# Routed experts: eleven batches routed early instead of twelve, list ends on the sync queue, late scatters three to a unit, and the 176 inner columns in two halves of 88

## The chip, the cores and the metric

The kernel runs on one core of one Trainium2 chip. The metric is the device time of one execution in microseconds, the median of several runs. The program is written as one instruction stream per engine (TensorE, VectorE, ScalarE, GpSimd and SyncE), which wait for each other by semaphores.

## The reference, cut to what matters

The reference is a decoder of two layers on 16 batches of 128 tokens of width 256. Layer 0 has attention, cross attention and a feed-forward; layer 1 has windowed attention, cross attention and routed experts. The change touches the last part and, through its first steps, the two attentions ahead of it.

```python
shared_out = silu_and_mul(xf @ shared_w1.T) @ shared_w2.T        # inner width 352
probs = softmax(xf @ gate_w.T)                                   # 16 experts
routing_weights, selected = top_k(probs, 6)
gate_up = einsum('th,eoh->teo', xf, w1)                          # inner width I = 176 for each expert
act = silu(gate) * up
moe_out = einsum('te,tei,ehi->th', combine, act, w2)
x = layernorm(x + moe_out + shared_out)
```

There are 2048 tokens, each goes to 6 of the 16 experts.

## The kernel before, in words

All values are float32. The routed part is not computed densely. Every expert has a list of token rows in memory (`spread`); a token's row (its 256 values, its number and its 16 weights, 273 values) is written to six lists by indirect transfers, six scatters for a batch of 128 tokens. Then 111 tiles of 128 rows are read back from the lists, each tile belongs to one expert, and its result is added into memory by an indirect transfer that accumulates.

There are three stages at the end of the program.

1. *The two small attentions* (`small_attentions`, function `overlapped`). The orders of the pieces on each engine are written out by hand in `SELF_ORDERS` and `CROSS_ORDERS` (lines 1675 to 1701), as names with a lag in batches. `EarlyRouting` puts the router of batches 0 to 11 there, in three groups of four: logits, six best, positions in the lists (class `Router`), and the scatters (`scatter0` to `scatter5`, line 2497) on GpSimd. At the stage's end SyncE waits for all scatters, and all engines meet at a barrier (line 109).
2. *The shared stage* (first part of `routed_feed_forward`). Four groups of four batches pass the shared expert in three units each (128, 128 and 96 of 352 columns), twelve units `q`. TensorE makes gate and up (line 3162), ScalarE the silu (3266), VectorE the product (3351), TensorE projects (3173) two units later. Between groups TensorE turns the next tokens (3143) and ScalarE copies them out (3253). The router of the last four batches runs beside it (lines 2281 to 2360); GpSimd then issues 24 scatters (3115) and 16 list ends (3119), indirect transfers that fill the 128 slots behind each list with empty rows. `tables` and `tables_back` (3319 to 3343) work out which expert and which rows each tile has.
3. *The tile loop*, 111 tiles. SyncE reads the rows (3095). TensorE works in rounds: turn the rows of tile i (3203), gate and up of tile i-1 (3217), turn the product of tile i-2 (3225, 3226), result of tile i-3 (3232, 3233). The inner width of 176 stands across partitions as 128 + 48: two transposes, two copies out (3402, 3403), and two matmuls that accumulate:

```python
pe.matmul(p_y[i % 2][:, 0:H], actT[i % 2][:, :], weights.w2[:, bass.ds(e * H, H)], start=True, stop=False)
pe.matmul(p_y[i % 2][:, 0:H], actT_low[i % 2][:, :], weights.w2_low[:, bass.ds(e * H, H)],
          start=False, stop=True).then_inc(y_made, 1)
```

GpSimd adds the result into one of two buffers in memory in turn (3127) and waits before each for the one two tiles earlier to have landed (`done_of(i - 2)`). A float32 matmul is two passes, so the trace has two instructions for one `matmul` call.

Of the kernel before, what the change touches and what calls it, by code (L numbers as in the profile page):

```python
# [1273 lines left out]
def x0_attend(core, kT, svu, rsv, vraw, ahead):  # L1274
# [10 lines left out]
    with ExitStack() as ctx:  # L1285
# [323 lines left out]
        def _(dve):  # L1609
# [620 lines left out]
EI, SI = 176, 352  # L2230
GROUP = 4
# [7 lines left out]
EARLY = 3  # L2239


class Router:

    SIZES = (("logit", GROUP * EXPERTS), ("prob", GROUP * (EXPERTS + 2)), ("repl", GROUP * (EXPERTS + 2)),
             ("chosen", GROUP * EXPERTS), ("order", GROUP * EXPERTS), ("count0", GROUP * (PAD + EXPERTS)),
             ("count1", GROUP * (PAD + EXPERTS)), ("slotf", GROUP * EXPERTS), ("pick", CHOICES * GROUP * EXPERTS),
             ("slot", CHOICES * GROUP), ("info", GROUP * (1 + EXPERTS)), ("rstat", 3 * GROUP), ("best", GROUP * 8))
    ROOM = sum(n for _, n in SIZES)  # L2250
    STEPS = 1 + 4 + 1 + GROUP + 1 + 1 + 1

    def __init__(self, core, weights, sem, room, first, groups):
        self.core, self.weights, self.first, self.groups = core, weights, first, groups
        at = {}
        for name, n in self.SIZES:
            lo = sum(m for _, m in self.SIZES[:len(at)])
            at[name] = room[:, lo:lo + n]

        def by_group(name):  # L2260
            return at[name].rearrange("p (g e) -> p g e", g=GROUP)
# [5 lines left out]
        self.pick = at["pick"].rearrange("p (k g e) -> p k g e", k=CHOICES, g=GROUP)  # L2267
        self.slot_all, self.slot = at["slot"], at["slot"].rearrange("p (k g) -> p k g", k=CHOICES)
# [4 lines left out]
            "c_steps", "info_up", "slots_up"))  # L2273

# [5 lines left out]
    def shifted(self, dve, n, logits):  # L2280
        dve.tensor_reduce(self.rstat[:, 0, :], logits, AX.X, ALU.max).then_inc(self.r_max, 1)
        dve.wait_ge(self.r_max, n + 1)
        dve.tensor_tensor(self.logit, logits, bcast(self.rstat[:, 0, :], [P, GROUP, EXPERTS]), ALU.subtract).then_inc(self.r_in, 1)

    def exponentials(self, act, n):
        act.wait_ge(self.r_in, n + 1)
        act.wait_ge(self.ready, 3)
        after(act, self.info_up, n)
        act.activation(self.prob[:, :, 0:EXPERTS], self.logit, ACT.Exp).then_inc(self.r_exp, 1)

    def choose(self, dve, n):
        rstat, prob, repl, best = self.rstat, self.prob, self.repl, self.best
        pr = prob[:, :, 0:EXPERTS]
        dve.wait_ge(self.ready, 3)
        dve.wait_ge(self.r_exp, n + 1)
        dve.tensor_reduce(rstat[:, 1, :], pr, AX.X, ALU.add).then_inc(self.r_steps, 1)
        dve.wait_ge(self.r_steps, 3 * n + 1)
        dve.reciprocal(rstat[:, 2, :], rstat[:, 1, :]).then_inc(self.r_steps, 1)
        dve.wait_ge(self.r_steps, 3 * n + 2)
        dve.tensor_tensor(pr, pr, bcast(rstat[:, 2, :], [P, GROUP, EXPERTS]), ALU.mult).then_inc(self.r_steps, 1)  # L2300
# [3 lines left out]
        for j in range(GROUP):  # L2304
            dve.wait_ge(self.r_best, GROUP * n + j + 1)
            dve.match_replace(repl[:, j, :], best[:, j, :], prob[:, j, :], CHOSEN).then_inc(self.r_repl, 1)
        dve.wait_ge(self.r_repl, GROUP * (n + 1))
        dve.tensor_scalar(self.chosen, repl[:, :, 0:EXPERTS], CHOSEN, None, ALU.is_ge).then_inc(self.chosen_up, 1)

    def describe(self, dve, n):  # L2310

        lo = (self.first + n) * GROUP
        dve.tensor_copy(self.info[:, :, 0], self.weights.token[:, lo:lo + GROUP])
        dve.scalar_tensor_tensor(out=self.info[:, :, 1:], in0=self.repl[:, :, 0:EXPERTS], scalar=CHOSEN, in1=self.prob[:, :, 0:EXPERTS],
                                 op0=ALU.is_ge, op1=ALU.mult).then_inc(self.info_up, 1)

    def rank(self, pe, n, bank):
        pe.wait_ge(self.chosen_up, n + 1)
        m = GROUP * EXPERTS
        pe.matmul(bank[:, 0:m], self.weights.earlier[:, :], self.picked, start=True, stop=True)  # L2320
        pe.matmul(bank[:, m:2 * m], self.weights.every[:, :], self.picked, start=True, stop=True).then_inc(self.ranked, 1)

    def positions(self, dve, n):

        at = self.STEPS * n
        dve.wait_ge(self.chosen_up, n + 1)
        dve.tensor_copy(self.count[0][:, :, PAD:], self.chosen).then_inc(self.c_steps, 1)
        for i, s in enumerate((1, 2, 4, 8)):
            dve.wait_ge(self.c_steps, at + 1 + i)
            dve.tensor_tensor(self.count[(i + 1) % 2][:, :, PAD:], self.count[i % 2][:, :, PAD:],  # L2330
                              self.count[i % 2][:, :, PAD - s:PAD + EXPERTS - s], ALU.add).then_inc(self.c_steps, 1)
        dve.wait_ge(self.c_steps, at + 5)
        dve.tensor_tensor(self.order, self.count[0][:, :, PAD:], self.chosen, ALU.mult).then_inc(self.c_steps, 1)

    def take(self, dve, n, bank):

        base, at, w, lo = self.weights.base, self.STEPS * n + 6, GROUP * EXPERTS, (self.first + n) * GROUP
        dve.wait_ge(self.weights.ones_up, 2)
        dve.wait_ge(self.ranked, n + 1)
        for j in range(GROUP):  # L2340
# [3 lines left out]
        dve.tensor_tensor(self.slotf, base[:, lo:lo + GROUP, :], bank[:, 0:w].rearrange("p (g e) -> p g e", e=EXPERTS),  # L2344
# [1170 lines left out]
```

## Time and profile before

| | us |
|---|---|
| runs, median of 3 | 2864.49 (2857.27 to 2869.05) |
| the profiled execution | 2860.28 |
| its span | 2858.4 |
| mean granted clock of TensorE | 0.933 |
| TensorE busy | 2400.8 (84%) |
| VectorE busy | 1886.4 (66%) |
| ScalarE busy | 1596.1 (56%) |
| GpSimd busy | 733.2 (26%) |

Times in the profile are microseconds from the span's start. PE is TensorE's matmuls, PEld its weight loads, DVE VectorE, ACT ScalarE, POOL GpSimd, SPq SyncE's queue. "<-" behind an instruction's idle time names what ended it; "issue" is time in which nothing that is recorded held it, "remote" a release that no recorded instruction explains. The small attentions end at 2382.6, the shared stage runs from there to 2503, the tile loop to about 2823, and the last sums and norms to the end. The share of busy time over the whole span tells little here, since each stage is limited by something else; the stretches and chains below are to be read stage by stage.

### The profile page before, as it was taken

The page shows a single profiled execution, that of the slowest core. Times are in us where ns is not written, and L with a number is a line of the kernel's source. Part 1 is how long each engine was busy: PE and PEld are TensorE (multiplying, and loading weights), DVE is VectorE, ACT ScalarE, POOL GpSimd, SP SyncE. Part 2 cuts the span into 40 slices and gives each one's busy share as a digit, 9 for nine tenths or more (in the row PEclk, how much of TensorE's full clock was granted, in tenths as well). Part 3 has the DMA queues.
Part 4 walks back from the last instruction along what each step waited for, and adds up shares of the span by engine and source line. Part 5 has one row for each costly group of instructions (what it writes and reads, how often), then busy time and mean ns, then how long its engine had stood idle before and what let it go on. Part 6 is the DMA issues. An engine that isn't in the chain of part 4 may idle for free. (4 is left out here: it accounts for less than half of the span.)

```text
span 2858.4 us, 50647 instructions
## 1 busy us (share of the span) xinstructions
PE 2400.8 (84%) x16545; PEld 1519.7 (53%) x16545; DVE 1886.4 (66%) x4500; ACT 1596.1 (56%) x3092; POOL 733.2 (26%) x913
## 2 busy tenths in 40 slices
PE   6999999999976577777777799799979765599995
PEld 3766667676753344444444455455556543355552
DVE  5778787777747899999999322466657652134443
ACT  3666665656643799989999311466646541033332
POOL 1121212121201222222222000111112664245554
PEclk9999999999997899989999899999999987799997
DMA  5000000000000899999999500400000113156665
GB/s 191 1 1 0 0 0 0 0 0 0 0 23 23 173 186 184 181 173 188 178 179 184 115 1 0 142 1 1 1 7 12 65 64 106 54 96 97 98 97 135
DMA packets 537921, 211.18 MB, mean 74 GB/s; under 512 B 475012, under 2 KB 531840, under 8 KB 536704
## 3 DMA queue, kind: packets, MB, share of 16 engines
q1 hardware_dynamic: 515952, 178.30, 31.0%
q0 software_dynamic: 21360, 30.22, 6.0%
q8 instruction: 113, 1.85, 0.3%
q14 instruction: 80, 0.66, 0.1%
q10 hardware_dynamic: 416, 0.16, 0.0%
HBM read 54.27 MB, written 36.90 MB: 32 GB/s over the span
## 5 line engine op out<-in xcount | busy, mean ns | idle before, releaser
L1651 DVE TENSOR_SCALAR_CACHE_REDUCE x_row<-x_p_s,x_nsq 128x1024 f32<-128x1024 f32 x512 | 621.7, 1274 | 28.7 <-PE x_p_s L1427 28.7
L1520 ACT ACTIVATE x_ints<-x_row,x_nb 128x2048 uint16<-128x2048 f32 x256 | 511.7, 2000 | 41.9 <-DMA x_turned<-x_ints 20.7
L1427 PE MATMUL x_p_s<-x_kT,x_qz 128*128 128x512 bf16 x1024 | 321.0, 409 | 131.5 <-DVE x_row L1651 126.9
L363 POOL TENSOR_TENSOR a_rstd<-a_ssq,neghalf 128x16 f32<-128x16 f32 x32 | 126.0, 3936 | 522.0 <-DVE a_ssq L874 522.0
L3127 POOL DMA_INDIRECT f_acc<-f_yt,f_ids x111 | 171.9, 1548 | 201.9 <-ACT f_yt L3290 200.6
L1427 PEld LDWEIGHTS x_p_s<-x_kT,x_qz 128*128 128x128 bf16 x1024 | 72.3, 101 | 268.0 <-DVE x_row L1651 242.1
L1554 POOL TENSOR_SCALAR x_nb<-x_low,x_hmin 128x1 f32<-128x1 f32 x256 | 75.0, 293 | 498.4 <-DVE x_row L1651 497.1
L1461 PEld LDWEIGHTS x_p_o<-x_vi,x_turned 128*128 128x128 f16 x4096 | 144.0, 98 | 87.2 <-DMA x_turned<-x_ints 18.3
L2095 ACT COPY s_eT<-sc_p_e 128x512 f32<-128x512 f32 x192 | 112.3, 585 | 132.4 <-PE sc_p_e L1985 131.5
L1461 PE MATMUL x_p_o<-x_vi,x_turned 128*128 128x16 bf16 x4096 | 143.0, 170 | 17.1 <-DMA x_turned<-x_ints 17.0
L3217 PE MATMUL f_p_g<-f_w,f_rowsT 128*128 x444 | 151.0, 463 | 0.0
L1985 PE MATMUL sc_p_e<-ident,s_e 128*128 128x128 f32 x768 | 124.4, 286 | 30.6 <-ACT s_eT L2095 17.6
L3402 DVE COPY f_actT<-f_p_u 128x128 f32<-128x128 f32 x111 | 32.4, 291 | 170.2 <-issue 149.9
L704 ACT ACTIVATE a_prob<-a_p_work,a_nbias,a_rqs 128x128 f32<-128x128 f32 x256 | 114.3, 463 | 36.7 <-DVE a_nbias L983 36.7
L1985 PEld LDWEIGHTS sc_p_e<-ident,s_e 128*128 128x128 f32 x768 | 86.1, 144 | 75.6 <-issue 58.4
L450 PE MATMUL a_p_proj<-a_wq,a_xT 128*128 128x512 f32 x256 | 123.7, 608 | 2.7 <-DMA a_wq<-in_L_attn_Wq_dram 2.7
L570 PE MATMUL a_p_o<-a_wo,a_cT 128*128 128x256 f32 x512 | 120.9, 379 | 0.0
L450 PE MATMUL a_p_proj<-a_wk,a_xT 128*128 128x512 f32 x256 | 117.6, 593 | 0.0
L2889 DVE TENSOR_TENSOR f_h<-f_act_g,f_p_u 128x512 f32<-128x512 f32 x32 | 22.0, 688 | 138.1 <-PE f_p_y L2791 123.3
L450 PE MATMUL a_p_proj<-a_wv,a_xT 128*128 128x512 f32 x256 | 112.7, 592 | 0.3 <-ACT a_cv L663 0.3
L2083 ACT ACTIVATE s_e<-s_e 128x1024 f32<-128x1024 f32 x96 | 100.1, 1059 | 13.5 <-DVE s_e L2181 10.8
L2172 DVE TENSOR_REDUCE s_rmax<-sc_p_s 128x8 f32<-128x1024 f32 x64 | 76.6, 1217 | 45.3 <-PE sc_p_s L1968 45.3
(462 smaller groups left out, 5484.7 us busy)
## 6 DMA issues: line engine op xcount, KB each, us to landing
f_rows<-f_spread SPq DMA_DIRECT2D x111, 136.5 KB
f_w<-in_L_ffn_w_dram SPq DMA_DIRECT2D x2, 2816.0 KB, 13.1
x_turned<-x_ints SPq DMA_TRANSPOSE x224, 4.8
f_sum<-f_acc SPq DMA_DIRECT2D x6, 512.0 KB, 7.1
x_res<-in_x_dram SPq DMA_DIRECT2D x2, 1024.0 KB, 7.1
a_wq<-in_L_attn_Wq_dram SPq DMA_DIRECT2D x2, 1024.0 KB, 10.8
a_wk<-in_L_attn_Wlk_dram SPq DMA_DIRECT2D x1, 2048.0 KB, 18.5
a_wv<-in_L_attn_Wlv_dram SPq DMA_DIRECT2D x1, 2048.0 KB, 10.8
```

The source lines that it names most:

```text
L363: pool.tensor_tensor(rstd[:, hs], ssq[:, hs], core.neghalf[:, 0:NH], ALU.pow).then_inc(root_h.sem, 1)
L450: mm = pe.matmul(proj[n % 2][:, :], xT[:, t, :], w_qkv[i][:, t, c * BANK:(c + 1) * BANK], start=(t == 0), stop=(t == KT - 1))
L570: mm = pe.matmul(p_o[:, 0:H], cT[g % 2][:, h, :], w_o[:, g * G + h, :], start=(g == 0 and h == 0), stop=(g == NG - 1 and h == G - 1))
L704: i = act.activation(prob[g % 2][:, h, :], work[g % 2][:, h * P:(h + 1) * P], ACT.Exp, bias=nbias[:, n:n + 1], scale=rqs[:, n:n + 1], accu ...
L1427: mm = pe.matmul(p_s[n % SLOTS][:, c * BANK:(c + 1) * BANK], qz[b % 2][:, par, a, :], kT[:, a, at:at + BANK], start=True, stop=True)
L1461: mm = pe.matmul(p_o[:, h * XD:(h + 1) * XD], turned[k][:, c, :].bitcast(F16), vi[:, c, h * XD:(h + 1) * XD], start=(c == 0), stop=(c == B ...
L1520: act.activation(ints[k][:, :], rows[k][:, :, :].rearrange("p s n -> p (s n)"), ACT.Exp, bias=nb[:, k:k + 1], scale=-1.0, accum_out=esum[: ...
L1651: dve.tensor_scalar(rows[k][:, half, :], p_s[n % SLOTS][:, :], nsq[:, b % 2, h:h + 1], HIGHEST, ALU.mult, ALU.min, accum_out=(low if half ...
L1985: mm = pe.transpose(s.p_e[:, j * P:(j + 1) * P], s.e[(b * s.PAIRS + g // 2) % 4][:, g % 2 * G + j, :], core.ident[:, :])
L2095: act.copy(s.eT[g % 4][:, :, :].rearrange("p g k -> p (g k)"), s.p_e[:, :]).then_inc(s.eT_up.sem, 1)
L3127: pool.indirect_dma_start(acc[i % 2], bass.IndirectOffsetOnAxis(ap=ids[i % YR][:, :], axis=0), yt[i % YR][:, :], None, compute_op=ALU.add) ...
L3217: mm = pe.matmul(p_g[i % 2][:, 0:2 * EI], rowsT[i % 2][:, t * P:(t + 1) * P], weights.w1[:, t, bass.ds(e * (2 * EI), 2 * EI)], start=(t == ...
```

## The change

Four things are changed together.

- `SPANS` replaces groups of equal size: groups of 4, 4 and 3 batches are routed in the small attentions, the last five batches in the shared stage. The logits of batch 11 are still made early and kept in `left`. In GpSimd's order the six scatters of a batch stand two, two and two instead of three, one, one and one. Six scatters fewer are issued early, six more late.
- The 16 list ends move from GpSimd's indirect transfers to SyncE: plain transfers whose address is read from a register.
- The 30 late scatters wait for the gates of the units, three for each (`paced`). The ranking matmuls move from behind unit 1 to behind unit 0, and numbering stands ahead of the first product; the tables are read back at unit 9 instead of 11.
- The 176 inner columns are held as two halves of 88: weights, transposes and matmuls have 88 partitions each, and one copy of 88x256 replaces two.

```diff
+HALF = EI // 2
-EARLY = 3
+SPANS, REST = ((0, 4), (4, 4), (8, 3)), (11, 5)
...
-    "pool": [("spread1", 1), ("scatter3", 9), ("residual", 0), ("root_qk", 0), ("scatter4", 9), ("spread0", 0), ("scatter5", 9),
-            ("norm_root", 3), ("scatter0", 8), ("scatter1", 8), ("scatter2", 8)],
+    "pool": [("spread1", 1), ("scatter2", 9), ("scatter3", 9), ("residual", 0), ("root_qk", 0), ("scatter4", 9), ("scatter5", 9),
+            ("spread0", 0), ("norm_root", 3), ("scatter0", 8), ("scatter1", 8)],
...
-        self.w2, self.w2_low = sb("w2", [P, EXPERTS * H]), sb("w2_low", [low, EXPERTS * H])
+        self.w2 = [sb(f"w2{j}", [HALF, EXPERTS * H]) for j in range(2)]
...
+        def paced(m):
+            return 1 + m // 3
...
             sp.dma_start(spread[EXPERTS * CAP:, :], empty[:, :]).then_inc(dump_in, 16)
+            sp.wait_ge(empty_up, 2)
+            for e in range(EXPERTS):
+                at = sp.value_load(empty_at[0:1, e:e + 1], min_val=0, max_val=SLOTS - P)
+                sp.dma_start(spread[bass.ds(at, P), :], empty[:, :]).then_inc(ends_in, 16)
...
-            for j in range(GROUP):
+            for j in range(LATE):
                 pool.wait_ge(staged_up, j + 1)
                 pool.wait_ge(router.slots_up, 1)
                 for k in range(CHOICES):
+                    pool.wait_ge(gate_made, paced(j * CHOICES + k))
...
-            pool.wait_ge(empty_up, 2)
-            for e in range(EXPERTS):
-                pool.indirect_dma_start(spread, bass.IndirectOffsetOnAxis(ap=empty_at[:, e:e + 1], axis=0),
-                                        empty[:, :], None).then_inc(ends_in, 16)
...
+                if not q:
+                    router.rank(pe, 0, p_x[1])
                 if q >= 2:
                     project(q - 2)
-                if q == 1:
-                    router.rank(pe, 0, p_x[1])
-                if q == total - 1:
+                if q == total - 3:
                     turn_tables()
...
-                pe.transpose(p_u[i % 2][:, 0:P], act_in[i % 2][:, 0:P], core.ident[:, :])
-                pe.transpose(p_u[i % 2][0:LOW, P:2 * P], act_in[i % 2][:, P:EI], core.ident[:, :]).then_inc(act_turned, 1)
+                for j in range(2):
+                    mm = pe.transpose(p_u[i % 2][0:HALF, j * P:(j + 1) * P], act_in[i % 2][:, j * HALF:(j + 1) * HALF], core.ident[:, :])
+                mm.then_inc(act_turned, 1)
...
-                pe.matmul(p_y[i % 2][:, 0:H], actT[i % 2][:, :], weights.w2[:, bass.ds(e * H, H)], start=True, stop=False)
-                pe.matmul(p_y[i % 2][:, 0:H], actT_low[i % 2][:, :], weights.w2_low[:, bass.ds(e * H, H)],
-                          start=False, stop=True).then_inc(y_made, 1)
+                for j in range(2):
+                    mm = pe.matmul(p_y[i % 2][:, 0:H], actT[i % 2][:, j * P:(j + 1) * P], weights.w2[j][:, bass.ds(e * H, H)],
+                                   start=(j == 0), stop=(j == 1))
+                mm.then_inc(y_made, 1)
...
-                dve.tensor_copy(actT[i % 2][:, :], p_u[i % 2][:, 0:P])
-                dve.tensor_copy(actT_low[i % 2][:, :], p_u[i % 2][0:LOW, P:2 * P]).then_inc(actT_up, 1)
+                dve.tensor_copy(actT[i % 2][:, :], p_u[i % 2][0:HALF, 0:2 * P]).then_inc(actT_up, 1)
```

The first place is one batch of the small attentions on GpSimd (c_kz at line 1866 is a "spread", x_res the residual, c_rstd and c_ln_r the two roots, the DMA rows are scatters). Before:

```order
L1852 TENSOR_TENSOR x_res<-x_res,c_bias_out 128x256
L1858 TENSOR_TENSOR c_rstd<-c_ssq,c_eps 128x2
L1860 TENSOR_TENSOR c_rstd<-c_rstd,neghalf 128x2
L2497 DMA f_spread<-s_kz,f_slots 34944x273
L1866 TENSOR_TENSOR c_kz<-c_qkT,c_owner 128x256
L2497 DMA f_spread<-s_kz,f_slots 34944x273
L1874 TENSOR_TENSOR c_ln_r<-c_mv,c_eps 128x1
L1876 TENSOR_TENSOR c_ln_r<-c_ln_r,neghalf 128x1
L2497 DMA f_spread<-s_kz,f_slots 34944x273 x3
L1866 TENSOR_TENSOR c_kz<-c_qkT,c_owner 128x256
L2497 DMA f_spread<-s_kz,f_slots 34944x273
L1852 TENSOR_TENSOR x_res<-x_res,c_bias_out 128x256
```

In the changed kernel (the lines of the scatters are 2521 there):

```order
L2521 DMA f_spread<-s_kz,f_slots 34944x273 x2
L1852 TENSOR_TENSOR x_res<-x_res,c_bias_out 128x256
L1858 TENSOR_TENSOR c_rstd<-c_ssq,c_eps 128x2
L1860 TENSOR_TENSOR c_rstd<-c_rstd,neghalf 128x2
L2521 DMA f_spread<-s_kz,f_slots 34944x273 x2
L1866 TENSOR_TENSOR c_kz<-c_qkT,c_owner 128x256
L1874 TENSOR_TENSOR c_ln_r<-c_mv,c_eps 128x1
L1876 TENSOR_TENSOR c_ln_r<-c_ln_r,neghalf 128x1
L2521 DMA f_spread<-s_kz,f_slots 34944x273 x2
L1866 TENSOR_TENSOR c_kz<-c_qkT,c_owner 128x256
```

Three scatters ahead of the second spread became two, and two stand together behind the root of q and k.

The second place is the end of the small attentions and the rest of the program on GpSimd. Before:

```order
L2497 DMA f_spread<-s_kz,f_slots 34944x273 x6
L1874 TENSOR_TENSOR c_ln_r<-c_mv,c_eps 128x1
L1876 TENSOR_TENSOR c_ln_r<-c_ln_r,neghalf 128x1
L2497 DMA f_spread<-s_kz,f_slots 34944x273 x12
L2512 UNCONDITIONAL_BRANCH
L108 ISA x3
L3108 UNCONDITIONAL_BRANCH
L3110 MEMSET f_sum 128x1024
L3115 DMA f_spread<-f_staged,f_slots 34944x273 x24
L3119 DMA f_spread<-f_empty,f_empty_at 34944x273 x16
L3127 DMA f_acc<-f_yt,f_ids 2176x256 x111
```

In the changed kernel:

```order
L2521 DMA f_spread<-s_kz,f_slots 34944x273 x6
L1874 TENSOR_TENSOR c_ln_r<-c_mv,c_eps 128x1
L1876 TENSOR_TENSOR c_ln_r<-c_ln_r,neghalf 128x1
L2521 DMA f_spread<-s_kz,f_slots 34944x273 x6
L2536 UNCONDITIONAL_BRANCH
L108 ISA x3
L3140 UNCONDITIONAL_BRANCH
L3142 MEMSET f_sum 128x1024
L3148 DMA f_spread<-f_staged,f_slots 34944x273 x30
L3156 DMA f_acc<-f_yt,f_ids 2176x256 x111
```

The last twelve early scatters became six, the 24 late ones 30, and the 16 list ends are gone from this engine.

The third place is one round of the tile loop on TensorE. Before (f_w is the wide part of the weights, f_w_low the 48 rows):

```order
L3225 MATMUL f_p_u<-ident,f_act 128x128
L3226 MATMUL f_p_u<-ident,f_act 48x128
L3232 ISA
L3232 MATMUL f_p_y<-f_w,f_actT 128x256
L3233 REGISTER_ALU
L3233 MATMUL f_p_y<-f_w_low,f_actT_low 128x256
L3203 MATMUL f_p_x<-ident,f_rows 128x128 x2
```

In the changed kernel:

```order
L3255 MATMUL f_p_u<-ident,f_act 88x128 x2
L3263 ISA
L3263 MATMUL f_p_y<-f_w,f_actT 128x256
L3263 REGISTER_ALU
L3263 MATMUL f_p_y<-f_w,f_actT 128x256
L3232 MATMUL f_p_x<-ident,f_rows 128x128 x2
```

The same number of passes stands in the same order; 128 and 48 partitions became 88 and 88.

## Rows read from the trace of the kernel before

**Rows 1.** Stretches: us, busy PE PEld DVE ACT POOL (count), clock, DMA share, GB/s.

```profile
2432.00:2453.00 21.00, 0.00 (x0) 0.00 (x0) 0.68 (x1) 0.00 (x0) 16.12 (x17) 0.50 0.30 113
2620.00:2720.00 100.00, 100.00 (x425) 59.80 (x425) 42.00 (x210) 37.29 (x106) 55.01 (x36) 1.00 0.60 97
```

**Rows 2.** Timeline of the standstill: start, us, engine, line, operation, [idle before <-releaser].

```profile
2424.75 0.59 ACT L3266 ACTIVATE f_act_g<-f_p_g 96x512 f32<-96x512 f32 x1 [10.93 <-remote]
2452.15 0.68 DVE L3351 TENSOR_TENSOR f_h<-f_act_g,f_p_u 96x512 f32<-96x512 f32 x1 [31.71 <-remote]
2459.07 1.07 ACT L3253 COPY f_xT<-f_p_x 128x512 f32<-128x512 f32 x2 [33.73 <-remote]
2460.20 3.78 PE L3162 MATMUL f_p_g<-f_xT,f_sg 128*128 128x512 f32 x4 [36.78 <-ACT f_xT L3253]
2480.45 1.98 PE L3162 MATMUL f_p_g<-f_xT,f_sg 128*128 128x512 f32 x4 [1.16 <-ACT f_xT L3253]
```

**Rows 3.** Late scatters and list ends by line: ns min/median/max, first and last start.

```profile
L3115 POOL DMA_INDIRECT f_spread<-f_staged,f_slots x24: 959/963/967, 2402.8 to 2432.0; - x24
L3119 POOL DMA_INDIRECT f_spread<-f_empty,f_empty_at x16: 959/963/964, 2433.2 to 2452.2; - x16
```

**Rows 4.** DMA queues from 2418.6 to 2424.8: packets, MB, share.

```profile
q8 instruction: 1, 0.02, 1.0%
```

**Rows 5.** Timeline of POOL and PE at the border of the two stages.

```profile
2354.51 2.07 PE L2027 MATMUL sc_p_out<-c_w_o,s_oT 128*128 128x256 f32 x4 [0.46 <-issue]
2358.84 1.17 POOL L2497 DMA_INDIRECT f_spread<-s_kz,f_slots  x1 [0.19 <-issue]
2372.99 0.96 POOL L2497 DMA_INDIRECT f_spread<-s_kz,f_slots  x1 [0.30 <-issue]
2382.58 0.95 POOL L3110 MEMSET f_sum<- 128x1024 f32 x1 [8.63 <-POOLq L109]
```

**Rows 6.** Waits from 2225 to 2340, then 2340 to 2384: us, times, longest.

```profile
PE sc_p_s L1960 <- POOL c_kz L1866: 11.3, 5, 2.6
POOL c_kz L1866 <- ACT c_qkT L2077: 13.2, 7, 3.9
ACT s_oS L2107 <- remote: 3.8, 1, 3.8
```

**Rows 7.** Timeline, start of the shared stage: the choice, and unit 1 on TensorE.

```profile
2392.00 0.20 DVE L2308 TENSOR_SCALAR f_room<-f_room 128x64 f32<-128x64 f32 x1
2394.84 1.88 PE L3162 MATMUL f_p_g<-f_xT,f_sg 128*128 128x512 f32 x4
```

**Rows 8.** Chain of waits through one round of the tile loop.

```profile
2642.07 1.19 PE f_p_g L3217 x4
2643.47 0.43 PE f_p_y L3232 x2
2643.90 0.63 PE f_p_y L3233 x2
2644.53 0.37 PE f_p_x L3203 x2
2644.90 1.19 PE f_p_g L3217 x4
```

**Rows 9.** Chain of waits in the shared stage: a projection of 96 rows.

```profile
2489.32 1.73 PE f_p_y L3173 x8
```

**Rows 10.** Timeline of the tile loop: the weight loads of 48 rows.

```profile
2621.16 0.29 PEld L3233 LDWEIGHTS f_p_y<-f_w_low,f_actT_low 48*128 48x128 f32 x2 [0.33 <-issue]
```

**Rows 11.** Chain of waits behind the loop: an accumulation into memory.

```profile
2820.71 3.99 DMA f_acc<-f_yt,f_ids
2824.76 0.69 issue
```

**Rows 12.** SyncE, row transfers at a register address: ns min/median/max.

```profile
L3094 SPq TENSOR_LOAD <-f_row_of x111: 262/268/770, 2502.0 to 2809.1; - x111
L3095 SPq DMA_DIRECT2D f_rows<-f_spread x111: 337/338/379, 2503.2 to 2809.8; - x111
```

More of the change, by code:

```diff
@@ L2273, in __init__, with earlier_ones @@
             "c_steps", "info_up", "slots_up"))
+    def earlier_ones(self, n):
+        return sum(m for _, m in self.spans[:n])
     def start(self, dve):
@@ L2382, in __init__, with span_of @@
         self.turn, self.small = other.p_out[:, H:2 * H], other.p_out[:, H:H + EXPERTS]
-        self.batches = EARLY * GROUP
+        self.batches, self.looked = REST[0], REST[0] + 1
+    def span_of(self, b):
+        return sum(b >= lo + m for lo, m in SPANS)
     def tensor(self, pe):
@@ L2398, in logits @@
         def logits(b):
-            if b < s.batches:
+            if b < s.looked:
                 if not b:
@@ L2407, in rank @@
         def rank(b):
-            if b < s.batches and b % GROUP == GROUP - 1:
+            if b in s.last:
                 pe.wait_ge(s.read, b + 1)
@@ L2411, in rank @@
                 pe.wait_ge(s.weights.ones_up, 2)
-                s.router.rank(pe, b // GROUP, s.turn)
+                s.router.rank(pe, s.last[b], s.turn)
         return {"r_turn": turn, "r_logits": logits, "r_rank": rank}
     def free(self, pe, b):
-        after(pe, self.read, min(b - 1, self.batches))
-        after(pe, self.router.taken, min((b - 6) // GROUP + 1, EARLY))
+        after(pe, self.read, min(b - 1, self.looked))
+        after(pe, self.router.taken, sum(b >= at + 3 for at in self.last))
     def scalar(self, act):
@@ L2433, in logits_up @@
         def logits_up(b):
-            if b < s.batches:
+            if b < s.looked:
                 act.wait_ge(s.made, b + 1)
-                after(act, s.router.r_in, b // GROUP)
-                act.copy(s.raw[:, b % GROUP, :], s.small).then_inc(s.read, 1)
+                n = s.span_of(b)
+                after(act, s.router.r_in, n)
+                dst = s.raw[:, b - SPANS[n][0], :] if b < s.batches else s.weights.left[:, 0, :]
+                act.copy(dst, s.small).then_inc(s.read, 1)
         def exponentials(b):
-            if b < s.batches and b % GROUP == GROUP - 1:
-                s.router.exponentials(act, b // GROUP)
+            if b in s.last:
+                s.router.exponentials(act, s.last[b])
         def stage(b):
@@ L2457, in run @@
             def run(b):
-                if b < s.batches and b % GROUP == GROUP - 1:
-                    piece(b // GROUP)
+                if b in s.last:
+                    piece(s.last[b])
             return run
@@ L3087, in _ @@
             sp.wait_ge(dump_in, 16)
-            for i in range(GROUP):
+            for i in range(LATE):
                 sp.wait_ge(spread_in[i], 16 * CHOICES)
@@ L3257, in stage @@
                 act.wait_ge(router.info_up, 1)
-                for j in range(GROUP):
-                    act.copy(staged[j][:, 0:H], core.x[:, EARLY * GROUP + j, :])
+                for j in range(LATE):
+                    act.copy(staged[j][:, 0:H], core.x[:, BEFORE + j, :])
                     act.copy(staged[j][:, H:], router.info[:, j, :]).then_inc(staged_up, 1)
@@ L3367, in _ @@
             router.positions(dve, 0)
+            router.take(dve, 0, p_x[1])
+            router.number(dve, 0)
             for q in range(total):
```

152 lines of the change are left out of this document (82 added, 70 removed).

## The prediction, made before the changed kernel ran

> **What bounds the kernel now.** I read the busy time by stretch first, then the timeline where a stretch is empty, then the chain of waits through the stage that is left. The reader is to see three different things in the last 500 us.
>
> The shared stage (all tokens through the shared expert, twelve units) has a hole. From 2432 to 2453 TensorE works 0.00 us of 21 and ScalarE not at all, while GpSimd is busy for 16 of them [rows 1]. The timeline names the instructions: ScalarE's activation of 2424.75 had waited 10.93 us, VectorE's product of 2452.15 waited 31.71, ScalarE's copy of 2459.07 waited 33.73, all "remote", which means that no recorded instruction released them; TensorE then waited 36.78 us for that copy [rows 2]. TensorE had ended its last work at 2460.20 - 36.78 = 2423.4, so the later two had their inputs 25 to 35 us before they ran. What ran meanwhile was GpSimd's row of indirect transfers: 24 scatters from 2402.8 and 16 list ends until 2452.2 [rows 3]. One fetch of instructions is recorded just before 2424.8, where ScalarE went on [rows 4]. So I take the hole as instruction pages that come late while GpSimd issues indirect transfers without a pause. That is an inference: for the two longer waits no fetch is recorded.
>
> The border before the shared stage is set by GpSimd alone. TensorE ends at 2356.58, twelve scatters start from 2358.84 to 2372.99, and the new stage starts at 2382.58 [rows 5].
>
> The tile loop is TensorE's: 100.00 us busy of 100, clock 1.00, GpSimd at 55 [rows 1]. One round is 2644.90 - 2642.07 = 2.83 us, and 111 rounds are 314 us [rows 8].
>
> **The change, part by part.** The sum is made against the profiled execution's 2860.28 us (span 2858.4), which is 4.2 us under the median of the runs, 2864.49.
>
> *Border.* Eleven batches instead of twelve are scattered early. Behind the last early root there are 6 scatters instead of 12, as the order rows show. One costs (2372.99 - 2358.84) / 11 = 1.286 us, so the border comes 6 x 1.286 = 7.7 us earlier. The last scatter then ends at about 2366.2, still behind TensorE's 2356.58, so GpSimd stays the last and the gain counts whole; the 9.6 us from the last scatter to the new stage stay. In the same place ScalarE has one "remote" wait of 3.8 us beside twelve scatters in a row [rows 6]; it may go or stay (0 to 3.8), and I take 2.
>
> *Order on GpSimd in the early part.* Three scatters before spread1 become two, and scatter 5 moves ahead of spread0. TensorE waited 11.3 us in five batches for that product of GpSimd [rows 6]; this is the most that can come back. Against it: spread0 has one more scatter ahead, 1.286 us, but GpSimd idled 13.2 / 7 = 1.9 us there waiting for ScalarE [rows 6], which covers it. Were that cover gone it would cost 11 x 1.286 = 14.1. Between -11.3 and +14.1 I take -7, near the row that shows the cover.
>
> *Shared stage.* What the hole costs: 36.78 us, less the 1.16 that every turn of a new group leaves there, and the first projection at half clock (3.78 us against 1.98) [rows 2]: 35.6 + 1.8 = 37.4 us. The clock row over the empty stretch is 0.50, so TensorE starts again at 1.2 GHz [rows 1]. The change issues the thirty late scatters three to a unit; a unit is three pieces of 1.73 us [rows 9], 5.2 us, so GpSimd issues for 3.9 us and then pauses. Six go at once at the start, since unit 1 is under way when the slots are known. The last three wait for the tenth gate of twelve, two units or 10 us before TensorE's end, against 3.99 us for an indirect transfer to land [rows 11]; nothing is late for the first tile's rows. The pacing also limits itself: a unit that stands still releases no more scatters. What stays dense is SyncE's part: sixteen list ends at 0.268 + 0.338 us or more each [rows 12], 10 to 18 us, on hardware queues and beside at most nine scatters. The bounds are 0 and -37.4; I leave 4 us of waiting and take -33.4.
>
> The rest of this stage I cost at nothing. The added waits: ranking now waits behind unit 0 for the choice, and unit 1 stands behind it on TensorE; the choice of four batches was made at 2392.2 and unit 1 started at 2394.84 [rows 7], so 2.6 us cover the fifth batch and two small copies. Behind the paced scatters GpSimd has only the accumulations, which need the first tile anyway; numbering before the first product delays that product, whose buffer TensorE wants only in unit 2; the tables and the 111 x 16 owner compare move from unit 11 to unit 9, behind nothing that TensorE waits for. If this cover were gone it would be some single microseconds. SyncE's sixteen list ends stand ahead of its stores of x, which nothing before the loop needs.
>
> *Tile loop.* In the round the two passes of 128 rows (line 3232) take 0.43 us, the two of 48 rows (line 3233) 0.63, and the two transposes behind them 0.37; the two transposes before 3232 take 2643.47 - 2643.26 = 0.21 [rows 8]. Same columns, so 0.20 and 0.16 us are extra, and they stand around the 48-row step only: its weight load starts 0.33 us after the one before ended [rows 10]. A 96-row projection in the shared stage pays nothing: eight passes in 1.73 us, 0.216 each, as fast as the 0.43 / 2 of line 3232 [rows 8, 9]. Halves of 88 rows are nearer to 96. Saved: 0.36 x 111 = 40.0 us; I take 38, because the first and last rounds are not steady. Bounds: 0, if 88 behaves as 48 (a loss is excluded, since the passes and their columns are the same), and -40.0. VectorE's one copy of 88x256 for two copies is beside the path: TensorE leaves no gap there.
>
> The page "TensorEngine Tiling (Array Packing)" of the Trainium skill (section Tiling Modes) says that a change of tiling mode drains TensorE, and lists modes of 128, 64 and 32 rows. By it 48 rows would be a 64-row mode and both 88 and 96 the full one; the rows agree as far as 48 and 96 go. No run here shows 88.
>
> Sum: 7.7 + 2 + 7 + 33.4 + 38 = 88.1; 2860.3 - 88.1 = 2772.2, and with the 4.2 to the median **2776 us**. After the loop I expect nothing to change.
>
> **Rivals.**
> A. *The hole stays, fed by SyncE.* The starving is by the amount of transfers, not by who issues them; the sixteen list ends and the first six scatters then stand closer together than before. For it: the transfers and their bytes are as many as before. Against: the DMA engines were only 0.30 busy in the hole and 0.60 in the loop, which has no such wait [rows 1]. Price: the 37.4 us stay, 2776 + 33.4 = 2809.
> Beside it, the page "DMA: Bandwidth & Descriptors" of the skill (section Issuing engines are not separate DMA queues) says that DMAs of SyncE and GpSimd end on the same 16 engines, so moving the issue saves sequencer time alone; that speaks for A. The busy share in rows 1 does not bear it out.
> B. *88 rows pay as 48 do.* The loop gives nothing: 2776 + 38 = 2814. Against it is the 96-row row.
> C. *The accumulation becomes the bound.* Each of two memory buffers takes the next tile only when its last one has landed: 3.99 + 0.69 us for two tiles [rows 11], 2.34 us per tile, against the new round of 2.47. The margin is 0.13 us. The DMA share would rise from 0.60 to 0.69; if landing grows to 4.6, the tile takes 2.65 and the loop gives 20 us: 2794.
> D. *Every burst starves the engines by itself; this is the way to a slower kernel.* ScalarE went on 6.9 us after the last list end started [rows 2, 3]. If each of ten bursts holds ScalarE and VectorE from its first scatter until then, 2 x 1.286 + 6.9 = 9.4 us, and TensorE restarts at half clock (1.8), ten bursts cost 112 us instead of 37.4. With the other terms (54.7 gained) that is 20 us slower: 2884. It decides from 9.2 us per burst. Against it: in the early part six scatters per batch, three in a row, go with no remote wait in the list of 2225 to 2340; the one of 3.8 us comes in the stretch after it [rows 6], where they stand in runs of six and twelve.
>
> **Chances.** Forecast 0.60; A 0.16; C 0.10; B 0.07; A and B together 0.04 (2847); D 0.03. The forecast's own range is 2756 (all terms at their best, 100.2 us, and the spread of the runs) to 2795. The range reaches over A and B to 2820 and leaves out the last two. A measurement of this kernel tells about 0.5% from no change, 14 us, so the limits are 2850 and 2879. Faster 0.95 (the first four and half of A with B), same 0.02, slower 0.03.
>
> **What would show it.** Border: six scatters behind the last root and the first transpose of the new stage between 2362 and 2375, near 2366. Hole: no "remote" wait above 5 us in the shared stage, and the scatters in threes. If it is still there, whether it falls beside SyncE's sixteen (A) or beside each three (D). Loop: rounds of 2.47 us in the chain, the four result passes 0.86 us together; a round of 2.83 is B, and GpSimd waiting for its own transfer is C. I am wrong in the large if the hole moves elsewhere instead of going, since that term and the loop carry 71 of the 88 us.

## The result, and the profile after

The changed kernel takes 2773.11 us (median of 4 runs, 2769.67 to 2785.46) beside 2860.88 of the kernel before: ratio 0.970, 95% interval 0.966 to 0.974. On another chip the pair was timed again: 0.969, 0.968 to 0.970. The forecast was 2776. The span of the profiled execution is 2770.3 us, so 88.1 us went, which is to the tenth the forecast's sum; the table shows that its terms missed in both directions.

| stretch | before | after | gone | forecast |
|---|---|---|---|---|
| start to the first c_rstd (L1858) of the cross attention | 2111.4 | 2114.7 | -3.3 | 0 |
| from there to the last stage's MEMSET | 271.2 | 251.9 | 19.3 | 7.7 + 2 + 7 = 16.7 |
| shared stage, to the first transposes of rows | 122.7 | 84.9 | 37.8 | 33.4 |
| tile loop, to the last ones | 309.3 | 275.8 | 33.5 | 38 |
| rest of the span | 43.8 | 43.0 | 0.8 | 0 |

The first row is no effect: the second profile of the changed kernel has 2109.2 there, that of the kernel before 2112.2.

*The border.* The timeline of the changed kernel's GpSimd answers to [rows 5]: the first and the last of the six scatters behind the last root, and the new stage at 2366.59 where it was 2382.58 (the forecast said near 2366).

```profile
2351.52 1.16 POOL L2521 DMA_INDIRECT f_spread<-s_kz,f_slots  x1 [0.19 <-issue]
2358.05 0.96 POOL L2521 DMA_INDIRECT f_spread<-s_kz,f_slots  x1 [0.30 <-issue]
2366.59 0.95 POOL L3142 MEMSET f_sum<- 128x1024 f32 x1 [7.58 <-POOLq L109]
```

*The shared stage.* The stretches of the changed kernel, with the columns of [rows 1], from the first late scatter on, and in the loop. TensorE is busy for 19 us of 21 while GpSimd issues nearly as densely as in the old hole (15 transfers and 13.89 us busy against 17 and 16.12).

```profile
2384.00:2405.00 21.00, 19.01 (x65) 11.04 (x64) 5.85 (x19) 3.45 (x6) 13.89 (x15) 1.00 0.50 172
2600.00:2700.00 100.00, 99.57 (x479) 73.21 (x478) 46.11 (x199) 38.13 (x119) 61.87 (x40) 1.00 0.65 109
```

The twelve scatters that are released at once (the slots are known only when four gates have been made) still leave a trace. In the timeline ScalarE's gate had its input from the pass of 2395.53, which ended at 2397.4. VectorE's first product had its inputs earlier still. Both engines go on together at 2400.6, 2.2 us after the twelfth issue ended. TensorE has work for that long and loses next to nothing.

```profile
2395.53 1.88 PE L3191 MATMUL f_p_g<-f_xT,f_sg 128*128 128x512 f32 x4
2400.58 0.60 ACT L3297 ACTIVATE f_act_g<-f_p_g 128x512 f32<-128x512 f32 x1 [7.70 <-DMA x_wp<-in_L_xattn_Wp_dram]
2400.62 1.33 DVE L3382 TENSOR_TENSOR f_h<-f_act_g,f_p_u 128x512 f32<-128x512 f32 x2 [12.39 <-PE f_p_u L3191]
```

The releaser "x_wp" is a load from long ago: the trace has no fitting release there either, under another name.

*The loop.* The chain of waits through one round answers to [rows 8]; the round is 2642.47 - 2639.98 = 2.49 us (forecast 2.47).

```profile
2639.98 1.19 PE f_p_g L3246 x4
2641.16 0.22 PE f_p_u L3255 x2
2641.38 0.86 PE f_p_y L3263 x4
2642.25 0.22 PE f_p_x L3232 x2
2642.47 1.19 PE f_p_g L3246 x4
```

The timeline has the weight loads of 88 rows back to back, without the idle 0.33 of [rows 10]:

```profile
2641.11 0.73 PEld L3263 LDWEIGHTS f_p_y<-f_w,f_actT 88*128 88x128 f32 x4
```

### The profile page after: what moved, and what is told of

Its sections match the earlier page's. It is cut to its first block and busy times, and to the rows that moved or that the text cites. A ratio compares the mean times of both kernels' runs of the same rounds, so it can differ in the third digit from the quotient of the medians.

```text
span 2770.3 us, 50620 instructions
## 1 busy us (share of the span) xinstructions
PE 2359.1 (85%) x16545; PEld 1537.1 (55%) x16545; DVE 1883.0 (68%) x4391; ACT 1585.0 (57%) x3092; POOL 715.0 (26%) x897
## 5 line engine op out<-in xcount | busy, mean ns | idle before, releaser
L3436 DVE COPY f_actT<-f_p_u 88x256 f32<-88x256 f32 x111 | 46.7, 421 | 130.8 <-PE f_p_u L3255 97.8
L3263 PE MATMUL f_p_y<-f_w,f_actT 88*128 x444 | 114.2, 379 | 0.0
L2083 ACT ACTIVATE s_e<-s_e 128x1024 f32<-128x1024 f32 x96 | 100.0, 1058 | 13.3 <-DVE s_e L2181 12.5
## 6 DMA issues: line engine op xcount, KB each, us to landing
a_wq<-in_L_attn_Wq_dram SPq DMA_DIRECT2D x2, 1024.0 KB, 11.3
```

What stands on the lines that cost most here:

```text
L3263: mm = pe.matmul(p_y[i % 2][:, 0:H], actT[i % 2][:, j * P:(j + 1) * P], weights.w2[j][:, bass.ds(e * H, H)], start=(j == 0), stop=(j == 1))
```

## Experiments

Times compare with the kernel before on the same chip. The chips were of two kinds, which was not expected. On at least three of them, and where the first two profiles come from, the kernel before takes 2854 to 2870 us, on two others 2814 to 2829. I call them chips of kind 1 and kind 2. Each was used in one short stretch of time only, so what differs may lie in the chip or in something else that held for that stretch.

### What makes the hole

Five kernels differ in how many indirect transfers GpSimd issues without a pause in the shared stage, and in who issues the list ends. All five ran on chips of kind 1.

**e1_no_pace**: the changed kernel with

```diff
 def paced(m):
-    return 1 + m // 3
+    return 1
```

> The changed kernel, but the thirty late scatters all wait for the first gate only, so they follow each other without a pause (the list ends stay with SyncE). Theory: an unbroken run of indirect transfers on GpSimd holds up the instructions of the other engines. Thirty of them in a row take 38.6 us where the kernel before had forty in 49.4; I expect a hole of 30 / 40 x 37 = 28 us, 2773 + 28 = 2801 us, with waits named remote above 5 us in the shared stage. Rival: the sixteen list ends on GpSimd made the hole; then it stays away, 2773. Rival A of the prediction (the amount of transfers counts, whoever issues them): about 2773 + 0, since the changed kernel has the same amount and no hole.

Measured: 2799.49 us (0.977, 0.974 to 0.979). The shared stage takes 112.0 us, 27 more than after. VectorE and ScalarE stand through most of the row of thirty (2389.8 to 2427.6), and TensorE for the 12.79 us in which it waits for VectorE, as its timeline shows:

```profile
2423.93 0.69 DVE L3382 TENSOR_TENSOR f_h<-f_act_g,f_p_u 128x512 f32<-128x512 f32 x1 [29.37 <-issue]
2424.67 3.73 PE L3191 MATMUL f_p_u<-f_xT,f_su 128*96 128x512 f32 x4 [12.79 <-DVE f_h L3382]
2432.24 1.08 ACT L3297 ACTIVATE f_act_g<-f_p_g 128x512 f32<-128x512 f32 x2 [30.05 <-DMA x_wp<-in_L_xattn_Wp_dram]
```

**e2_ends_gpsimd**: the changed kernel, list ends back on GpSimd behind the paced scatters.

```diff
 @block.sync:   -for e in range(EXPERTS): value_load(empty_at ...); dma_start(spread[bass.ds(at, P), :], empty)
 @block.gpsimd: +for e in range(EXPERTS): indirect_dma_start(spread, empty_at[:, e:e + 1], empty)
```

> The changed kernel, but the sixteen list ends are indirect transfers of GpSimd again, in one run behind the last paced scatter (2433 to 2453 us). Theory of the unbroken run: sixteen in a row take 20 us; TensorE has its last 12 us of the stage there, so a hole of 5 to 15 us and the first row transfer some 5 us later for the ends, 2780 to 2790. If the run must be longer than sixteen to hurt, only the later ends count: 2776 to 2780. If the list ends as such made the hole, it is 20 us or more: 2793 or more.

Measured: 2791.59 (0.975, 0.973 to 0.977), a little above the 2780 to 2790 expected; shared stage 99.9 us, 15 more: 6.7 are the first rows, for which TensorE now waits 11.98 us instead of 5.28, the rest stands beside VectorE's late last products and residual, for which TensorE's increments came up to 6.3 us late. The list ends follow the last three scatters without a pause, so the row at the end is one of nineteen (2437.0 to 2460.8), and the first one here was fifteen, not twelve.

**e3_ends_sync**: the kernel before, only the sixteen list ends moved to SyncE (the same lines as above, the other way round).

> The kernel before, with nothing changed but the sixteen list ends, now plain transfers of SyncE at a register address; the 24 late scatters stay one unbroken run of 31 us. Theory: the hole shortens by the 16 x 1.27 = 20 us that GpSimd's run is shorter, 2861 - 20 = 2841, waits named remote remain. Rival, the list ends made it: the hole is gone, 2861 - 35 = 2826. Rival A, the amount counts: no change, 2861.

Measured: 2843.07 (0.993, 0.991 to 0.995), shared stage 105.0 us. This is near the 2841 expected. Remote waits remain; this is the list of waits beside its row of 24:

```profile
ACT f_act_g L3266 <- remote: 27.6, 2, 14.2
DVE f_h L3351 <- remote: 8.6, 1, 8.6
```

**e4_paced**: the kernel before with pauses by unit, all forty still on GpSimd.

```diff
+def paced(m):
+    return 1 + m // 4
 for k in range(CHOICES):
+    pool.wait_ge(gate_made, paced(j * CHOICES + k))
     pool.indirect_dma_start(spread, ...)
 for e in range(EXPERTS):
+    pool.wait_ge(gate_made, paced(GROUP * CHOICES + e))
     pool.indirect_dma_start(spread, ... empty ...)
```

> The kernel before, with nothing changed but pauses: its 24 scatters and 16 list ends stay indirect transfers of GpSimd, each group of four waits for the gate of the next unit. Theory of the unbroken run: with pauses the hole is gone although GpSimd issues as much as before, 2861 - 35 = 2826. Rival, the list ends on GpSimd or the amount make it: it stays, 2850 to 2861. Four issues take 5.1 us and a unit 5.2, so it may also be that there is hardly a pause and the hole stays in part; then the timeline shows GpSimd busy from unit to unit.

Measured: 2840.16 (0.992, 0.989 to 0.994), not 2826. The doubt in the expectation came true: when the slots are known, several units' gates are made, and four issues last as long as a unit, so all 24 scatters went in one row (2403.9 to 2434.1) and made a hole of their own. The sixteen list ends behind them did pause (2443.8 to 2466.7) and no remote wait stands beside them.

**e12_before_pauses**: the kernel before with pauses that have no tie to the units.

```diff
     pool.indirect_dma_start(spread, ...)          # the 24 scatters and the 16 list ends alike
+    done += 1
+    if done % 3 == 0:
+        pool.memset(sums[0][1][:, :, :], 0.0).then_inc(paused, 1)
+        pool.wait_ge(paused, done // 3)
```

> The kernel before, its 24 scatters and 16 list ends still indirect transfers of GpSimd and all released at once, but after each three of them GpSimd clears a buffer of its own once (0.95 us and what stands around it). Nothing else is changed. The row gets some 17 us longer, 2403 to 2471 us, which may cost 3 us at the end of the stage. Theory of the unbroken run, where the kernel before takes 2861 us: its hole of 37 us goes, 2861 - 37 + 3 = 2827, ratio 0.988. Theory that the hole is a matter of the chip as well, where the kernel before takes 2817 to 2821 us: no hole is there to begin with, ratio 0.999 to 1.002; if the hole were there too, the ratio is 0.987 to 0.989. Rival: what helped the changed kernel was the tie to the units; then the ratio is 1.00 where the kernel before takes 2861 us too.

Measured: 2825.77 (0.987, 0.984 to 0.990), on a kind 1 chip, where 2827 was expected. The stretch of the old hole, once before [rows 1] and here: TensorE 19.84 us instead of 0.00, GpSimd busier than in the hole, and the DMA share 0.31 against 0.30.

```profile
2432.00:2453.00 21.00, 19.84 (x69) 11.96 (x68) 3.56 (x6) 2.86 (x5) 16.91 (x18) 1.00 0.31 112
```

So neither the amount of transfers nor the list ends make the hole, but the unbroken row, and pauses of 1.2 us after each three (0.97 us of clearing and 0.28 of wait) remove it whole. One rival is left: the pauses also thin the row out, forty issues in 62.6 us instead of 50.4, and no run slows the issues without pausing. The hole's size goes with the row's length. With 84 us taken as the stage without a hole, and the wait for the first rows taken out where it grew:

| GpSimd's longest row | kernel | shared stage | hole |
|---|---|---|---|
| 40 | before, two profiles | 122.7, 122.9 | 39 |
| 30 | e1 | 112.0 | 28 |
| 24 | e3, e4 | 105.0, 101.0 | 21, 17 |
| 19 (and one of 15) | e2 | 99.9, of it 6.7 later rows | 9 |
| 12 | after, two profiles | 84.9, 87.2 | 1 to 3 |
| 3 | e12 | 87.5, of it 4.3 later rows | 0 |

### What is late in the hole

The prediction took the waits for instruction pages. Two things speak against that. e3 and the kernel before have the same code on ScalarE, but other instructions stand: in e3 the fifth and sixth gate, in the kernel before the sixth gate and the third copy. And the trace also records when semaphores changed. For the four waits of [rows 2] and VectorE's one before them (kernel before; us):

```
increment by TensorE's          its matmul ended   change recorded   who goes on
third projection   (L3173)      2416.63            2418.43           VectorE 2418.55
sixth gate         (L3162)      2418.35            2424.73           ScalarE 2424.75
fourth projection  (L3173)      2422.54            2452.03           VectorE 2452.15
third turn         (L3143)      2423.41            2459.05           ScalarE 2459.07
```

Each engine goes on 0.02 to 0.12 us after the change: it had its instruction and waited for a number. The increment is what is late, by 1.8, 6.4, 29.5 and 35.6 us. (The ends of matmuls are modelled in these profiles, but TensorE had started its next pass each time, or, at 2423.4, could only wait.) They come through in the order of their matmuls: the sixth up pass, between the second and the third of the table, ended at 2420.07 and is recorded at 2432.43. The second profile of the kernel before (e11 below) repeats this, with 1.7, 4.2, 8.1, 22.5 and 35.7 us for the same five. Some changes in this stretch have no record, which does not make them late: the fourth gate ended at 2408.03, has no record, and ScalarE went on at 2408.07. TensorE, waiting for VectorE in e1, went on 0.05 us behind it, in the middle of the row, so not every engine's increment is late. SyncE shows the same disturbance in another way: by line, its small register steps, 152 ns as a rule, take up to 690 ns in the changed kernel and 1387 in e1, and never over 181 in a profile of a kind 2 chip (e9 below), in this order here (changed kernel, e1, e9):

```profile
L3112 SPq FUSED_REGOPS  x16: 3/152/690, 2383.9 to 2409.9; - x16
```

```profile
L3112 SPq FUSED_REGOPS  x16: 3/154/1387, 2390.2 to 2436.3; - x16
```

```profile
L3112 SPq FUSED_REGOPS  x16: 152/152/181, 2367.8 to 2384.6; - x16
```

Why increments are late is not settled, nor whether SyncE's slow steps and they have one cause.

### The other terms, on chips of kind 2

**e5_old_split**: the changed kernel with 128 + 48.

```diff
-self.w2 = [sb(f"w2{j}", [HALF, EXPERTS * H]) for j in range(2)]
+self.w2 = [sb(f"w2{j}", [(P, EI - P)[j], EXPERTS * H]) for j in range(2)]
-dve.tensor_copy(actT[i % 2][:, :], p_u[i % 2][0:HALF, 0:2 * P])
+dve.tensor_copy(actT[i % 2][0], p_u[i % 2][:, 0:P]); dve.tensor_copy(actT[i % 2][1], p_u[i % 2][0:EI - P, P:2 * P])
```

> The changed kernel with the inner columns in 128 and 48 again. The prediction's loop term: 0.36 us in each of 111 rounds comes back, 2773 + 38 to 40 = 2811 to 2813, rounds of 2.83 us. Rival: part of the gain was elsewhere, or rival C (the accumulation) had cut it short: then less than 35 comes back, 2800 to 2808. Rival B (88 rows pay as 48 do): 2773.

**e6_old_order**: the changed kernel, GpSimd's list in `CROSS_ORDERS` as before (scatter 2 behind scatter 1, scatter 5 behind spread0).

> The changed kernel with GpSimd's order of the kernel before in the part with the early scatters (three scatters between the two roots and spread 1, scatter 5 behind spread 0). The prediction's term: 7 us come back, 2780; TensorE's waits for the product c_kz (11.3 us in the kernel before) are there again and the last stage starts at 2373 instead of 2366.6. Rival: the order is worth nothing and the whole 16 us of the border came from six scatters fewer and what hangs on them: 2773.

**e7_groups_4444**: the changed kernel with

```diff
-SPANS, REST = ((0, 4), (4, 4), (8, 3)), (11, 5)
+SPANS, REST = ((0, 4), (4, 4), (8, 4)), (12, 4)
```

> The changed kernel with groups of 4, 4, 4 and 4 batches: twelve scattered early, four late, all else as changed. The prediction's border term: six scatters more behind the last root, 6 x 1.286 = 7.7 us, and up to 2 for a remote wait: 2781 to 2783, the last stage starts at 2374 to 2376. Rival: a row of twelve scatters at the border holds up the other engines as well and costs more than its issue: 2785 or more. Rival: the border is TensorE's and the scatters are covered: 2773.

**e9_pauses**: e1 with two clears after each three scatters.

> The changed kernel, its thirty late scatters released all at once by the first gate, but after each three of them GpSimd clears a buffer of its own twice (about 2 us), so that pauses stand in the row without any tie to TensorE's units. Theory of the unbroken run: the pauses alone are enough, no hole, 2773 to 2778. Rival: what helped was the tie to the units (a unit that stands still releases no more), or the row of thirty released together is bad in itself: 2790 to 2800, as without pauses.

All four ran on one chip, and their ratios go to the same kernel before, 2817.24 us, so the 2773 in the expectations is no base there. e9 is: it keeps the changed kernel's code but for the pauses in the shared stage, which takes 84.6 us in it.

| | us | ratio (interval) | L1858 to MEMSET | shared stage | loop |
|---|---|---|---|---|---|
| e9 | 2758.46 | 0.979 (0.977 to 0.982) | 238.7 | 84.6 | 279.1 |
| e5 | 2790.89 | 0.989 (0.987 to 0.992) | 239.2 | 84.5 | 310.5 |
| e6 | 2770.34 | 0.983 (0.981 to 0.985) | 257.1 | 84.2 | 280.2 |
| e7 | 2766.75 | 0.982 (0.980 to 0.983) | 251.2 | 83.5 | 277.5 |

- e5: the loop is 31.4 us longer than e9's and 34.7 than that of the first profile of the changed kernel; its steady round is 2.83 us again. By the medians of the runs, e5 lies 32.4 us above e9.
- e6: by the medians the old order costs 11.9 us; in the profile its stretch is 18.4 us longer, but the profiled execution was the slowest of five (2777.4 us; three took 2768 to 2770, two 2777). So the order is worth 12 to 18, not 7. TensorE's waits for the product are back, by the list of waits:

```profile
PE sc_p_s L1960 <- POOL c_kz L1866: 10.5, 6, 2.6
```

- e7: a twelfth early batch makes the first stretch 12.5 us longer, but the medians are 8.3 us apart, within the 7.7 to 9.7 expected: with one batch fewer to route late, the shared stage is 1.1 us shorter, and the rest (1.6 in the loop, 1.3 before the cross attention) is of the size by which profiles of the same code differ there.
- e9 says nothing on pauses, since this chip has no hole: its profile has no remote wait, and neither have the other three. In e5, e6 and e8 (below, also kind 2) the first eighteen scatters go in one unbroken row, 22.5 us long, and every increment of TensorE in the shared stage is recorded on time; on kind 1 a row of twelve already delays some. e12 tests the pauses.

**e10_changed_again** and **e11_before_again** are the two kernels without an edit, on a chip of kind 1 again.

> The changed kernel itself, without any edit, as a base for the runs with the old split, the old order, four equal groups, the pauses and the rows first, which stood beside a kernel before of 2817 to 2821 us instead of 2861. From the ratio found first (0.970) it would take 2733 there; if the chips differ only in the hole and the part with scatters, and the later kernels are what they should be, it takes about 2755: the rows first 2749 plus 4 to 7, the old split 2791 less 34 to 38, the equal groups 2767 less 7.7.

> The kernel before itself, without any edit, for a second profile. If its faster time beside the last five runs (2817 to 2821) is a smaller hole, the shared stage takes less than 105 us instead of 122.7 and the waits named remote there are fewer or shorter; if the difference lies elsewhere, that stage takes 118 to 123 us again and earlier stages are shorter.

Measured: 2773.23 (0.969, 0.968 to 0.970) and 2858.87 (0.999, 0.998 to 1.000). So neither kernel has a profile on kind 2. That the old hole is absent there is shown for rows of eighteen only; for the row of forty it is worked out: e9 stands 58.8 us below the kernel before, and the loop (32.4), the order (11.9) and the batch (8.3), all by medians, are 52.6 of it. That leaves 6.2 us, not 37. What the two show is how well a profile repeats: the old hole is there again (shared stage 122.9 us), and the changed kernel has one wait of 12.46 and one of 5.24 us, remote, beside its first twelve scatters (stage 87.2 us):

```profile
2395.17 1.34 DVE L3382 TENSOR_TENSOR f_h<-f_act_g,f_p_u 128x512 f32<-128x512 f32 x2 [12.46 <-remote]
2402.96 1.07 ACT L3284 COPY f_xT<-f_p_x 128x512 f32<-128x512 f32 x2 [5.24 <-remote]
```

In the profiles of the changed kernel and its variants the kinds differ only where GpSimd scatters. In the stretch from L1858 to MEMSET, which holds the early scatters, TensorE makes 297 increments. On kind 2 every one has a change recorded within 0.3 us of its matmul's end, in all five profiles. On kind 1 it is 286 and 288 of 297 in the kernel before, 263 and 264 in the changed one, whose stretch takes 251.9 us against 239 there. (The others are late or have no record.)

### A faster version

**e8_rows_first**: in the changed kernel SyncE's reads of the first rows stand behind its last store of x, which waits for the last residual; TensorE idles 5.28 us.

```diff
-for b in range(groups): keep(b)          # wait for res_up, store x
+for b in range(groups - 1): keep(b)
 for i in range(TILES):
+    if i == XR: keep(groups - 1)
     ... rows of tile i
-pe.wait_ge(res_up, groups)               # before the loop
+    if not i: pe.wait_ge(res_up, groups)  # in result(0)
```

> The changed kernel with two waits moved at the start of the tile loop: SyncE asks for the first four tiles' rows ahead of the last store of x (which waits for the last residual), and TensorE waits for that residual at its first result, not at its first transpose. In the changed kernel TensorE stands idle for 5.28 us before the first tile's transposes and runs its next passes at half clock. If the row transfers are what is late, 4 to 7 us go: 2766 to 2769. Rival: the accumulations, which need the last store of x, come later and the loop catches up on them: 2773.

Measured on a kind 2 chip: 2749.45 us, 0.974 (0.973 to 0.976) of 2820.89, the best ratio there (e9 0.979). Shared stage 79.0 us, 5.6 less than e9's, and in the loop's first transposes TensorE is at full clock (276 ns at most, 476 in the changed kernel):

```profile
L3237 PE MATMUL f_p_x<-ident,f_rows x222: 270/272/276, 2431.8 to 2708.2; 128*128 128x128 f32 x111
```

```profile
L3232 PE MATMUL f_p_x<-ident,f_rows x222: 270/274/476, 2451.5 to 2727.3; 128*128 128x128 f32 x111
```

It was not timed beside the changed kernel on one chip, so its gain of about 6 us rests on the stage's length; its median is 9.0 us under e9's, on another chip, and the other 3 us lie in the loop, where profiles of the same code differ by as much.

## Why the prediction was right

- *Where the hole is, its price, and that pauses end it*: right, and tested by e1, e3 and e12. The price of 37.4 is near the 39 of the table; it left out that the up pass behind the gate also ran at half clock (2.59 us instead of 1.88). Only 33.4 were claimed, to leave 4 for waiting; 37.8 went in the first pair of profiles and 122.9 - 87.2 = 35.7 in the second. The pacing was less than forecast: twelve scatters went at once, not six, and the sign that was named, no remote wait above 5 us, did not come true. The first profile has waits of 7.70 and 12.39 us under other names, the second two remote ones of 12.46 and 5.24; they cost little because TensorE had work meanwhile.
- *What the hole is*: wrong. It was read as late instruction pages, from one recorded fetch near the end of one wait. The late thing is TensorE's increments, by up to 35.6 us. Pauses were the remedy under either reading, which is why the error cost nothing.
- *Border and order, 16.7*: mis-sized, 19.3 and, in the second pair, 274.3 - 251.9 = 22.4 went. By the medians on kind 2 the batch's term (7.7 + 2) was right, with 8.3, and the order's (7) too small, with 11.9, about the whole of the wait of 11.3 us that the prediction took as the most that could come back; together 20.2, near what went on kind 1. The profiles have more in this stretch, 12.5 for the batch and 18.4 for the order, of which 10.5 is TensorE's wait; the rest is open, and e6's profiled execution was its slowest. The batch's term counted its six issues on GpSimd and no more, though with the batch its routing on the other engines moves as well. On kind 1 the changed kernel takes 13 us longer in this stretch than on kind 2; more of its increments are not on time there.
- *ScalarE's remote wait of 3.8*: 2 were claimed; one of 3.1 is still there.
- *Loop, 38*: 33.5 went, in the second pair 309.2 - 278.3 = 30.9. Per round 0.343 instead of 0.36, since the accumulating passes save 0.20 and the transposes 0.15: 38.1 for 111 rounds. The first ten rounds gain 1.2 us only (25.8 to 24.6). TensorE does not wait for rows there more than before (0.77 us against 0.65); it is at 1.2 GHz for longer, so that the third round lasts 2.80 us instead of 1.67. While TensorE waits 5.3 us for the first rows the granted clock falls to 0.50, in both kernels. It stays there from 2447.9 to 2458.2, 6.7 us into the loop, and in the kernel before from 2502.7 to 2509.6, 4.3 us into it. The stretches that begin 2.9 us into the loop, before and after, show the clock in the column behind GpSimd's:

```profile
2508.20:2512.00 3.80, 3.80 (x16) 2.38 (x15) 1.00 (x5) 1.28 (x4) 0.00 (x0) 0.82 0.02 5
2454.40:2458.00 3.60, 3.60 (x9) 2.04 (x8) 0.40 (x1) 0.69 (x2) 0.00 (x0) 0.50 0.05 16
```

A few later rounds of the changed kernel last 2.6 to 2.95 us; in the kernel before none of those is over 2.84. VectorE's waits for an accumulation to land rise from 0.3 us (2 of them) to 11.5 (26), so this looks like a small part of rival C: at 2.49 us a round has little slack left for GpSimd's transfers. Each pass of 88 rows takes 0.22 us, as one of 96 does, which excludes rival B. The page "TensorEngine Tiling (Array Packing)" of the Trainium skill (Tiling Modes), by which 88 rows would be a full mode like 96, agrees with that.
- *Rest of the stage at nothing*: held. Nothing that was moved behind another step shows as a new wait of TensorE, and the stage takes 83.5 to 84.6 us on kind 2 with this code, where no increment is late.
- *Rival A* (SyncE feeds the hole): SyncE's steps do get slower beside the first twelve scatters, 26 us for sixteen list ends against 17 in e9, but no engine stood for them; on its own terms e3 refutes it, since moving the ends shortened the hole by 18, and so does e12, where GpSimd issues all forty and the hole is gone. *Rival D* (each burst starves): a burst of twelve costs 1 to 3 us, of three nothing, far from 9.4.
- The exact sum is luck: +2.6, +4.4, -4.5, -3.3 and +0.8 us against the forecast cancel.

## What to carry to other kernels

Where GpSimd has many indirect transfers to issue beside a busy TensorE, look at every unbroken row of about ten or more for waits whose releaser is missing or absurd, and break the row: here a pause of 1.2 us after each three was enough, one spent on a useless clear. Compare when an engine goes on with when the matmul it waits for ended before blaming fetches or queues. When an effect is read from one profile, see first where its execution stands among the runs: e6's was 7 us above its median. And time such a change on several chips: the hole, 37 of the 88 us here, seems to exist only on some.

## What the runs showed of the hardware that was not expected

- The same program takes 2814 to 2829 us on two chips and 2854 to 2870 on the others. In the profiles of the changed kernel's code the difference lies in the stretches with GpSimd's indirect transfers alone: beside the early ones 297 of 297 increments recorded on time against 263 or 264, beside an unbroken row of eighteen no late one.
- Beside an unbroken row of such transfers on kind 1 increments of TensorE's matmuls arrived up to 35.7 us late and in the order of the matmuls, while one of VectorE's reached TensorE within 0.05 us, and some of SyncE's 152 ns steps took 0.7 to 1.4 us.
- The loss is about 1 us for each transfer of a long row (39 for 40, 28 for 30), less for shorter ones (17 and 21 for 24, 9 for 19 with one of 15), and 1 to 3 us for twelve.
